# The convolution stage worked in pairs of sequences inside the periods of the first attention, instead of as a block of its own

## What is computed

```
x0 = x @ W_in + b_in                       # 128 -> 384 features
q,k,v = causal depthwise conv, 3 taps, of x0
v  = causal depthwise conv, 4 taps, of k*v
x1 = layernorm(x + (q*v) @ W_out + b_out)  # the "mixer", first stage
a  = self-attention(x1), 16 heads of 64;   x = ln1(x1 + a)
a  = cross-attention(x, ctx), same shape;  x = ln2(x + a)
x  = ln3(x + fc2(gelu(fc1(x))));           x = layernorm(x1 + x)
x  = layernorm(x + experts(x))             # 16 token experts, one shared
```

## Time and profile before

| | us |
|---|---|
| median of three runs | 546.56 |
| lowest, highest | 544.33, 548.43 |
| the profiled execution's own time | 544.88 |
| its span, first to last instruction | 543.1 |
| PE busy | 475.7 (88% of the span) |
| DVE busy | 393.5 (72%) |
| ACT busy | 365.3 (67%) |
| POOL busy | 257.3 (47%) |

### The profile page before, as it was taken

How to read it: one execution, slowest core, us unless ns; L and a number is a source line. 1 busy time by engine, 2 the same in 40 slices (tenths; PEclk the granted TensorE clock), 3 DMA queues, 4 the chain that set the end, 5 groups by cost and what they waited for, 6 DMA issues and landing times. The chain is left out here.

```text
span 543.1 us, 13796 instructions
## 1 busy us (share of the span) xinstructions
PE 475.7 (88%) x4554; PEld 434.5 (80%) x4554; DVE 393.5 (72%) x1846; ACT 365.3 (67%) x1374; POOL 257.3 (47%) x321
## 2 busy tenths in 40 slices
PE   3857267899999999999999999999999998989482
PEld 2646156799999999999999999999999987878372
DVE  3378835777878877787888778788777776368964
ACT  3165436888877888887787888768888867535534
POOL 0338823345445455544544554454455546333661
PEclk9969669999999999999999999999999999999666
DMA  6580020000000000000000000000000000040003
GB/s 208 167 292 2 0 59 3 2 2 2 3 2 1 2 1 2 2 2 2 1 4 2 2 2 2 3 2 1 2 1 2 3 2 2 1 161 2 2 18 78
DMA packets 14166, 14.22 MB, mean 26 GB/s; under 512 B 2832, under 2 KB 11152, under 8 KB 13968
## 3 DMA queue, kind: packets, MB, share of 16 engines
q1 hardware_dynamic: 13952, 13.08, 8.0%
q10 hardware_dynamic: 144, 0.26, 0.1%
HBM read 12.16 MB, written 1.18 MB: 25 GB/s over the span
## 5 line engine op out<-in xcount | busy, mean ns | idle before, releaser
L729 ACT ACTIVATE P<-P,at_negmax 128x128 f32<-128x128 f32 x512 | 198.8, 395 | 80.2 <-DVE at_negmax L804 80.2
L903 POOL TENSOR_TENSOR P<-P,at_inv 128x512 f32<-128x512 f32 x128 | 131.7, 1041 | 132.5 <-DVE at_inv L814 132.3
L804 DVE CUSTOM_DVE_ANT_0 P<-late_bank,maskb 128x128 f32<-128x128 f32 x512 | 110.7, 287 | 1.7 <-PE late_bank L660 1.7
L830 DVE COPY at_PT<-late_bank 128x512 f32<-128x512 f32 x128 | 87.9, 688 | 33.0 <-PE late_bank L643 32.7
L729 ACT ACTIVATION_READ_ACCUMULATOR P<-P,at_negmax 128x1 f32 x512 | 99.4, 194 | 0.0
L643 PE MATMUL late_bank<-ident,P 128*128 128x128 f32 x512 | 76.3, 272 | 2.6 <-issue 1.8
L660 PE MATMUL late_bank<-at_k,at_q 64*128 64x128 f32 x1024 | 65.8, 278 | 2.2 <-DVE at_k L822 2.2
L643 PEld LDWEIGHTS late_bank<-ident,P 128*128 128x128 f32 x512 | 59.4, 140 | 8.6 <-issue 4.4
L660 PEld LDWEIGHTS late_bank<-at_k,at_q 64*128 64x128 f32 x1024 | 59.7, 188 | 6.2 <-issue 2.7
L672 PE MATMUL late_bank<-at_PT,V 128*64 128x128 f32 x1024 | 63.0, 276 | 0.0
L672 PEld LDWEIGHTS late_bank<-at_PT,V 128*64 128x64 f32 x1024 | 55.2, 137 | 3.9
(11 more groups left out here) (182 smaller groups left out, 1074.0 us busy)
## 6 DMA issues: line engine op xcount, KB each, us to landing
c_raw<-in_ctxT SPq DMA_DIRECT2D x1, 1024.0 KB, 11.5
out<-xres SPq DMA_DIRECT2D x4, 224.0 KB, 2.5
x<-in_xT SPq DMA_DIRECT2D x1, 768.0 KB, 5.9
tap_rows<-in_short_wT SPq DMA_DIRECT2D x3, 192.0 KB, 5.7
w_raw<-in_sa_wq SPq DMA_DIRECT2D x1, 512.0 KB, 12.3
w_raw<-in_sa_wk SPq DMA_DIRECT2D x1, 512.0 KB, 13.1
w_raw<-in_sa_wv SPq DMA_DIRECT2D x1, 512.0 KB, 10.7
w_raw<-in_ca_wq SPq DMA_DIRECT2D x1, 512.0 KB, 10.5
```

The source lines that it names most:

```text
L729: last = nc.scalar.activation(P[:, n % 2, h, :], P[:, n % 2, h, :], ACT.Exp, scale=-1.0, bias=negmax[:, n % 2, h:h + 1], accum_out=total[: ...
L804: last = nc.vector.tensor_tensor_reduce(P[:, n % 2, h, :], score_bank(h), k.maskb[:, cols(n)], scale=1.0, scalar=3.0e38, op0=ALU.add, op1= ...
L830: nc.vector.tensor_copy(PT[:, HQ * g:HQ * g + HQ, :], banks[T_BANK[g % 2]][:].rearrange("p (h l) -> p h l", h=HQ)).then_inc(pt_ok, 1)
L903: nc.gpsimd.tensor_tensor(tile, tile, inv[:, n % 2, HQ * g:HQ * g + HQ].unsqueeze(2).to_broadcast([128, HQ, 128]), ALU.mult).then_inc(norm ...
```

## The change

The mixer's block and the attentions' block become one block, with one order on each engine. The mixer works by pairs of sequences m (0 to 7; 256 columns a step) and is laid into the periods, which now begin at -7. Pair m has `projection` parts 0 and 1 in period 2m-6 and part 2 in period 2m-5; convolution, gate, output, residual, statistics, deviation, shift and normalisation in the even period 2m-4; its transposes, the split of `x1T` and the two additions in the odd period 2m-3. Attention's units begin in period -2 as before. The splits of the first three weights lie in periods -4 and -3, the mask in -2, the three weights of cross-attention in periods 1, 3 and 5, and the two halves of the context in 7 and 9.

The raw weights land in the tile of their own low half, so they need no slots and SP doesn't wait for one. The mixer's tiles share their space with those of the feed-forward, whose loads and `wo_ca` therefore wait for the end of the mixer. The banks of the mixer are those of the attentions: parts 0 and 2 of the projection in bank 4, part 1 and the transposes in bank 5, the output in bank 7.

The diff cut to its core (the stages' bodies keep their instructions, with PAIR in the place of GRP):

```diff
-RAW_SLOTS = 4
-FF_LOADS = 14
+FF_LOADS = 17
...
+        FIRST, FIRST_UNITS = -7, -2
...
+        def pair_of(p, lead):
+            m = (p + lead) // 2
+            return m if (p + lead) % 2 == 0 and 0 <= m < NPAIR else None
+
+        PROJECT, CONVOLVE, TRANSPOSE = 6, 4, 3
+        C_BANK, X1T_BANK = (4, 5, 4), 5
...
         def _(sp):
...
+            sp.dma_start(k.xres[:, 0:GRP], tokens[:, 0:GRP]).then_inc(ld_xres[0], 16)
+            for n in SA[:2]:
+                sp.dma_start(k.raw[n][:], io[n]).then_inc(ld_w[n], 16)
+            sp.dma_start(xT_raw[:, GRP:, :], io["xT"][:, GRP:, :]).then_inc(ld_x[2], 16)
+            sp.dma_start(k.raw[SA[2]][:], io[SA[2]]).then_inc(ld_w[SA[2]], 16)
+            for n, tile in k.rows.items():
+                row_broadcast(nc, sp, tile[:], io[n]).then_inc(ld_rows, 16)
+            sp.dma_start(k.xres[:, GRP:], tokens[:, GRP:]).then_inc(ld_xres[1], 16)
...
+            sp.wait_ge(x1lo, NPAIR)
+            sp.wait_ge(res1_ok, 2 * NPAIR)
+            sp.dma_start(k.wo_ca[:], ...)
+            load_feed_forward(k, sp)
...
+            def projection(p, m, c):
...
+                wait(pe, ot_ok, 2 * (p - 1))
+                wait(pe, c_ok, (3 * m, 3 * m, 3 * m + 1)[c])
...
+            def mixer_output(p, m):
...
+                pe.wait_ge(y_ok, m + 1)
+                wait(pe, xT_lo, p - 3)
...
             for p in range(FIRST, ITEMS + 1):
                 x_transpose(p - 4)
                 v_half(p, 0)
...
                 unit(p, 1)
                 v_half(p, 1)
                 transposes(p - 1, 1)
+                if p >= 0:
+                    mixer_output(p, pair_of(p, CONVOLVE))
                 unit(p, 2)
                 transposes(p - 1, 2)
+                projection(p, pair_of(p, PROJECT), 0)
+                projection(p, pair_of(p, PROJECT - 1), 2)
                 unit(p, 3)
                 transposes(p - 1, 3)
+                projection(p, pair_of(p, PROJECT), 1)
+                if p < 0:
+                    mixer_output(p, pair_of(p, CONVOLVE))
+                x1_transposes(p, pair_of(p, TRANSPOSE))
                 out_proj(p - 2)
                 scores(p + 1)
                 p_v(p - 1)
...
         def _(act):
...
             for p in range(FIRST, ITEMS + 1):
+                if p == -4:
+                    weight_high(SA[0])
                 exps(p, 0)
                 exps(p, 1)
...
                 v_out(p, 1)
+                projected(pair_of(p, PROJECT), 0)
+                projected(pair_of(p, PROJECT), 1)
+                projected(pair_of(p, PROJECT - 1), 2)
+                x1_high(pair_of(p, TRANSPOSE))
                 exps(p, 3)
+                if p == -4:
+                    weight_high(SA[1])
+                mixer_normal(pair_of(p, CONVOLVE))
+                if p % 2 and p >= -3:
+                    x_high((p + PROJECT + 1) // 2)
+                if p == -3:
+                    weight_high(SA[2])
+                elif p in (1, 3, 5):
+                    weight_high(CA[p // 2])
+                elif p in (7, 9):
+                    context_high((p - 7) // 2)
...
         def _(vec):
...
             for p in range(FIRST, ITEMS + 1):
                 maxima(p, 2)
                 maxima(p, 3)
                 normalise(p - 3)
+                inner_convolution(pair_of(p, CONVOLVE))
                 reciprocals(p, 0)
...
                 reciprocals(p, 2)
+                mixer_residual(pair_of(p, CONVOLVE))
                 pt_out(p - 1, 2)
                 k_out(p, 3)
                 pt_out(p - 1, 3)
+                mixer_statistics(pair_of(p, CONVOLVE))
...
+                x1_low(pair_of(p, TRANSPOSE))
                 residual(p - 2)
                 reciprocals(p, 3)
                 maxima(p + 1, 0)
                 maxima(p + 1, 1)
+                mixer_shift(pair_of(p, CONVOLVE))
...
+                if p % 2 and p >= -3:
+                    x_low((p + PROJECT + 1) // 2)
...
+                elif p in (1, 3, 5):
+                    weight_low(CA[p // 2])
+                elif p in (7, 9):
+                    context_low((p - 7) // 2)
...
         def _(pool):
...
             for p in range(FIRST, ITEMS + 1):
                 affine(p - 3)
                 next_residual(p - 3)
-                for g in range(QUARTERS):
+                normalise(p, 0)
+                gate(pair_of(p, CONVOLVE))
+                for g in range(1, QUARTERS):
                     normalise(p, g)
                 inverse_deviation(p - 2)
+                mixer_deviation(pair_of(p, CONVOLVE))
+                mixer_residuals(pair_of(p, TRANSPOSE))
+                keys_values(pair_of(p, PROJECT - 1))
+                output_bias(pair_of(p, PROJECT - 1))
...
-        setup_and_mixer(k)
         allocate_late(k, ctx)
-        attentions(k)
+        k.overlay(ctx, allocate_mixer_tiles, allocate_feed_forward)
+        mixer_and_attentions(k)
         feed_forward(k)
```

More of the change, by code:

```diff
@@ L80, in __init__, with overlay @@
         self.nc, self.io = nc, io
+        self.taken = 0
+        self.raw = {}
+    def overlay(self, ctx, early, late):
+        start = self.taken
+        with ExitStack() as before:
+            early(self, before)
+        wanted, self.taken = self.taken - start, start
+        late(self, ctx)
+        spare = wanted - (self.taken - start)
+        if spare > 0:
+            self.sb(ctx, early.__name__ + "_rest", [128, spare], U8)
     def sb(self, ctx, name, shape, dt=F32):
+        size = {F32: 4, F32R: 4, BF16: 2, U8: 1}[dt]
+        self.taken += -(-size * int(np.prod(shape[1:])) // 32) * 32
         return ctx.enter_context(self.nc.sbuf_tensor(name, shape, dt))
@@ L86, in split, with split_over_raw @@
         return Split(self.sb(ctx, name + "_hi", shape, F32R), self.sb(ctx, name + "_lo", shape, F32R))
+    def split_over_raw(self, ctx, name, shape):
+        taken = self.taken
+        with ExitStack() as before:
+            raw = self.sb(before, name + "_raw", shape)
+        self.taken = taken
+        lo = self.sb(ctx, name + "_lo", shape, F32R)
+        return Split(self.sb(ctx, name + "_hi", shape, F32R), lo), raw
     def banks(self, ctx, tag):
@@ L632, in v_half @@
                 wait(pe, v_ok, 2 * n + half)
+                if seq(n) == 0 and half == 0:
+                    wait(pe, w_lo, 3 * att(n) + 3)
                 mm_split(nc, banks[V_BANK][:], keys_T[att(n)], np.s_[:, cols(n)], values_w[att(n)],
@@ new lines, in x_high, with projected @@
+            def x_high(m):
+                if not 0 <= m < NPAIR:
+                    return
+                act.wait_ge(ld_x[min(m, 2)], 16)
+                wait(act, c_mm, 3 * (m - 1))
+                nc.scalar.activation(xT.hi[:, m % 2, :, 2:], xT_raw[:, seqs(m), :], ACT.Copy).then_inc(xhi, 1)
+            def projected(m, c):
+                if m is None:
+                    return
+                act.wait_ge(c_mm, 3 * m + c + 1)
+                wait(act, y_ok, m - 1)
+                if m == 0 and c == 0:
+                    act.wait_ge(bias_ok, 1)
+                nc.scalar.activation(C[:, m % 2, c], two(C_BANK[c]), ACT.Identity,
+                                     bias=bias[:, c:c + 1]).then_inc(c_ok, 1)
@@ new lines, in mixer_normal, with x1_high @@
+            def mixer_normal(m):
+                if m is None:
+                    return
+                act.wait_ge(shift1_ok, m + 1)
+                wait(act, xT1_mm, m)
+                wait(act, res1_ok, 2 * m)
+                for b in range(PAIR):
+                    last = nc.scalar.activation(N1[:, b], R1[:, b], ACT.Identity, bias=shift1[:, b:b + 1],
+                                                scale=rstd1[:, b:b + 1])
+                last.then_inc(n1_ok, 1)
+            def x1_high(m):
+                if m is None:
+                    return
+                act.wait_ge(xT1_mm, m + 1)
+                nc.scalar.activation(k.x1T.hi[:, pcols(m)], banks[X1T_BANK][:, 0:PCOLS], ACT.Copy).then_inc(x1hi, 1)
@@ new lines, in weight_high, with context_high @@
+            def weight_high(n):
+                act.wait_ge(ld_w[n], 16)
+                nc.scalar.activation(k.weights[n].hi[:], k.raw[n][:], ACT.Copy).then_inc(w_hi, 1)
+            def context_high(half):
+                act.wait_ge(ld_w["ctxT"], 16)
+                part = np.s_[:, half * T // 2:(half + 1) * T // 2]
+                nc.scalar.activation(k.ctxT.hi[part], k.raw["ctxT"][part], ACT.Copy).then_inc(ctx_hi, 1)
+            row_broadcast(nc, act, k.mask_raw[:], io["mask"].rearrange("b p -> (b p)")).then_inc(ld_mask, 16)
@@ new lines, in inner_convolution @@
+            def inner_convolution(m):
+                if m is None:
+                    return
+                vec.wait_ge(kv_ok, m + 1)
+                wait(vec, y_ok, m)
+                nc.vector.tensor_scalar(G[:], KV[:, :, 3:3 + L], inner[:, 3:4], inner_b[:, 0:1],
+                                        ALU.mult, ALU.add).then_inc(g_part, 1)
```

(4 more changed lines are left out.)

652 lines of the change are left out of this document (322 added, 330 removed).

## The result

The changed kernel takes 564.42 us (median of four runs, 563.07 to 566.48), the kernel before 545.84 on the same chip: a ratio of 1.034 [1.029, 1.039], slower. The prediction was 561, in 536 to 570. The profiled execution took 564.57, its span is 562.7 us.

A forecast was written before the change was run, and what follows sets the result against it. The mixer was bound by no engine, self-attention by PE. A gain of 41.6 us against 19.65 of PE work and 37.8 of waits took 544.88 to 560.7, given as 561, range 536 to 570.

The forecast's parts named there:

- S0: Start of item 0's scores, after the shortened mixer start: forecast 41.7 us, 41.6 earlier than before, bounds 38 and 47.
- Rival (c): First stage: loads arrive in the old rhythm and it waits 12 to 13 us: 574; chance 0.06 together with (d).
- Cost 1: PE-bound attention behind S0: projections, outputs and transposes of the mixer add 19.65 us of PE work, none hidden.
- Cost 2: Even periods: PE waits 4.1 us for yT, about 2.0 of it at the transposes; the period becomes 18.5 us.
- S: Start of scores(p) in a period, from which the forecast counts times within that period.
- Cost 3: Odd periods: normalisation delays `exps`; PE waits 2.0 us for V's eviction and 0.8 for a bank; period 15.95 us.
- Ramp: First periods after S0: period 0 forecast at 13.3 us, item 2's scores at 68.6, period 2 at 19.3 us.
- S12: Start of item 12's scores, after the mixer's last work: forecast 237.1 us against 221.3 before, 15.8 later.
- (a): Attention periods: waits hide, only PE's work stays: 523, faster; chance 0.22 together with what lies between 523 and 541.
- (b): Attention periods: ACT and DVE absorb half the waits, 19 us instead of 38: 542, no change to tell; chance 0.17.
- (d): Twelve periods: PE's gaps lower its clock, about 3 us each, 597; chance 0.06 together with Rival (c).
- The rule on the SBUF: Even periods: POOL's steps held behind DVE's convolution, gate 1.3 us later, 6.5 in all, 567; given 0.05.

The follow-up runs named there:

- e1: Changed kernel with DVE's low halves moved behind the copies of the probabilities: 560.27 us, ratio 1.029.
- e2: Changed kernel with ACT's mixer normalisation moved to the odd period, behind `v_out(p,1)`: 553.21 us, ratio 1.014.
- e5: Changed kernel with only the mixer's output product moved behind the fourth transposes, and its residual behind the last probability copy: 553.43 us, ratio 1.015.
- e6: e4 with x's rounded half made in the even period before and its remainder in the odd period: 530.85 us, ratio 0.973.
- e4: e3 with the mixer's output product moved behind the fourth transposes and its residual behind the last probability copy: 538.88 us, ratio 0.988.
- e3: Changed kernel with the moves of both e1 (low halves) and e2 (normalisation): 545.36 us, ratio 0.999.
- e8: Changed kernel with only POOL's two residual tensors moved earlier, behind the second normalisation of the same period: 560.11 us, ratio 1.027.
- e7: Changed kernel with only x's two halves moved earlier (even period before, then odd period): 564.68 us, ratio 1.036.

## Why the prediction was right, and where its sizes were off

**S0.** Forecast 41.7, measured 43.70. The step that was mis-sized: I had counted the wait of `mixer_normal` on ACT in odd periods from 1 on, and not in period -1, where the eviction of q stands behind it (1.4 us by e1 and e2), and not the fall of the clock behind it (1.1); the start of this execution was 0.6 earlier than theirs. e5 shows a second place that held S0, the residual ahead of `k_out` in period -2: it has 41.68 with the wait for q still there. The loads were in time: ACT splits sa_wq at 15.16, and from 0 to 43.7 us the one wait for a DMA is the first, for the taps. Rival (c) falls.

**Cost 1.** Too small. In e6, where PE hardly waits, an even period takes 15.10 and an odd one 13.48, so the added work is 3.2 and 1.6, not 2.55 and 1.25. Nine projection matmuls took about 1.18 (e4, 105.81 to 106.99), not 1.05, and even e6 keeps waits of 0.3. Over periods 0 to 11 e6 takes 28.6 us more than the kernel before, where I had 19.65 of work; some 3 us of the difference are waits (7.5 in its list, 4.5 before), and one drop of the clock is in it too.

**Cost 2.** Right in mechanism and place: the wait came in two pieces, 1.72 and 1.72, so 3.4 and not 4.1 in all; yT was done at S+11.48 (forecast 11.65). e5 and e6 take it away piece by piece, 18.4 to 16.8 to 15.1: its price is 3.3.

**Cost 3.** Right: `exps` began at S+4.54 (4.75), V was evicted at S+7.8 (8.5), PE waited 1.47 (2.0) and 0.43 (0.8). Its price by e2 is 2.34, not 2.8. In both costs the waits were sized too large and PE's work too small, so that 18.41 and 15.82 lie close to 18.5 and 15.95; this closeness is partly luck.

**Ramp.** The larger error: period 0 took 14.66 instead of 13.3 and period 1 15.75 instead of 13.6. What I left out is the clock. e5's period 0, without the wait for yT and without a drop, takes 10.90, so my 13.3 holds that wait but not the drop. In e1, period 1 at full clock takes 14.03. Period 2 took 18.13 instead of 19.3 and gave 1.2 back. The sum: S0 2.0, ramp 3.5, period 2 -1.2, all other periods -1.1, behind S12 0.5: 3.7 of the 3.9 by which the profiled execution (564.57) lies above 560.7.

**Rivals.** (a) and (b) fall, for the waits were not hidden: 29.9 us of them by the four rows of waits above, of the 37.8 forecast. Both outcomes exist as orders of the same work, though: e3 is (b) at 545, e6 comes near (a)'s 523 at 531, and the sign turns at e3, where the low halves and the normalisation have been moved. (d) I priced as a quarter of twelve periods and called unlikely for gaps of 2 us. It came in pieces: behind or within gaps of 1.0 to 2.3 us the clock fell, in one to four of twelve periods, for about 1.6 us each.

**The rule on the SBUF.** I had gone by the twelve equal runs of L412. They were no test: in the trace of the kernel before, POOL is idle beside them (it waits for G) or makes its deviation, a power of four columns. The changed kernel has the test. There POOL's 128x128 steps beside the convolution took 0.53 to 0.56 instead of 0.46, and the three `scalar_tensor_tensor` 1.78 together, and 1.53 at 17.36, where POOL is idle. The Trainium skill (SBUF — State Buffer, "Who interferes with whom") calls the ports that the two share an exclusive lock. Here that was worth some 0.25 us and not the 1.3 I had worked out from it, so the trace agrees in direction and not in size. For subtractions of two tensors in SBUF it agrees: x's remainder took 0.93 beside POOL's addition and 0.42 without it (e8).

## What to carry to other kernels

Work laid into the idle time of an engine can cost by its place in that engine's queue, whatever room the engine has in sum: here DVE and ACT had 20% room, and the wrong places cost 30 us, a few of them through the clock (periods 0 to 11 took 196.65 in the changed kernel and 166.56 in e6). Put instructions that nobody awaits behind those whose consumer is on the path, and never an instruction that itself waits for a chain over three engines ahead of them. When one wait is removed, read the list of waits again: e4 took yT's wait away and showed the one for x's remainder, and the moves of e6 together turned +3.4% into -2.7%.

## What was unexpected of the hardware

One drop of TensorE's clock in a busy stretch cost 1.6 us (e3, periods 6 and 8), and every changed kernel had one to four of them between S0 and S12, where the kernel before had none, all behind or within waits of 1.0 to 2.3 us, in different periods when the order changed. So an edit that saves less than 2 us can be cancelled by a drop elsewhere, as in e7; period by period its effect is still plain. The longest waits did not always lead to one: in period 10 a wait of 2.12 left the clock at 1.00 in the changed kernel, and behind one of 2.11 it fell in e2 (15.76 and 17.31 us).
